# A fourth looked-up tile in the edge-attention pass, and block marks made once per turn

## The reference, cut to what matters

```python
w = softmax(x @ attn_w.T + attn_b);  xp = x + w @ node_anchor
combined = concatenate([x[src], x[dst]], axis=1)
b = softmax(leaky_relu(combined @ edge_w.T + edge_b, 0.01), axis=1)   # (edges, 5)
ep = b @ edge_anchor
agg = zeros_like(xp).at[src].add(ep).at[dst].add(ep)
return xp + 0.5 * agg
```

## Time and profile before

| what | value |
|---|---|
| median of 3 runs | 5374.47 us (5369.51 to 5377.88) |
| profiled execution, its own time | 5368.31 us |
| span of the profiled execution | 5366.5 us |
| busy over the span: PE, POOL, DVE, ACT | 3267.3, 3069.5, 2026.5, 958.0 us |
| mean granted clock of PE over the span | 0.709 |

### The profile page before, as it was taken

One profiled execution on the slowest core, in us unless ns is written; L12 is line 12 of the kernel. 1 busy time (PEld: TensorE's weight loads), 2 busy tenths in 40 slices (PEclk: granted clock), 3 DMA queues, 4 the chain that ended last, 5 costly groups with the idle time before them and its releaser, 6 DMA issues. The chain is left out here.

```text
span 5366.5 us, 69161 instructions
## 1 busy us (share of the span) xinstructions
PE 3267.3 (61%) x19534; PEld 2183.4 (41%) x19535; DVE 2026.5 (38%) x6104; ACT 958.0 (18%) x2127; POOL 3069.5 (57%) x3180
## 2 busy tenths in 40 slices
PE   4357544558997555555554444444479955777777
PEld 2124322234444334334333333333334434666665
DVE  7441101033114322222222222222231157888886
ACT  0010000001003100000000000000010016888885
POOL 5777777730000577777776777777700006777773
PEclk8678767779998655555555555555589966888887
DMA  8521010113224422222222221222232202333322
GB/s 223 144 97 49 24 48 24 48 72 121 96 95 120 115 74 79 80 80 76 80 80 56 52 53 52 52 53 52 51 123 94 96 24 59 68 69 68 67 67 65
DMA packets 370426, 408.73 MB, mean 76 GB/s; under 512 B 89191, under 2 KB 305078, under 8 KB 360374
## 3 DMA queue, kind: packets, MB, share of 16 engines
q1 hardware_dynamic: 268854, 295.73, 17.2%
q0 software_dynamic: 101504, 112.13, 9.7%
HBM read 299.65 MB, written 107.98 MB: 76 GB/s over the span
## 5 line engine op out<-in xcount | busy, mean ns | idle before, releaser
L633 POOL DMA_INDIRECT GS<-xw_table,stage x1664 | 1571.9, 945 | 1182.7 <-issue 1109.9
L1120 PE MATMUL psum<-HA,HT 128*128 128x512 fp8e4 (+1 forms) x5733 | 1211.0, 373 | 458.3 <-DMA HA<-adj 411.6
L1072 PE MATMUL psum<-GS 128*128 128x96 f32 x3328 | 774.1, 409 | 1034.4 <-DMA GS<-xw_table,stage 1014.4
L1072 PEld LDWEIGHTS psum<-GS 128*128 128x128 f32 x3328 | 697.6, 310 | 1110.4 <-issue 1110.4
L633 POOL DMA_INDIRECT HA<-p_table,stage x676 | 652.2, 965 | 750.2 <-ACT stage L916 549.7
L667 POOL DMA_INDIRECT adj<-cell_value,cell_i x832 | 838.5, 1008 | 291.0 <-issue 249.1
L1120 PEld LDWEIGHTS psum<-HA,HT 128*128 128x128 bf16 x5733 | 549.7, 99 | 1093.7 <-issue 456.4
L1577 DVE TENSOR_TENSOR HA<-HA,psum 128x96 f32 x208 | 53.1, 255 | 1357.1 <-PE psum L1072 1357.1
L1563 DVE TENSOR_SCALAR GS<-iota,HT,wt 128x96 f32<-128x96 f32 x1680 | 434.9, 356 | 158.7 <-issue 157.7
L1831 DVE SCALAR_TENSOR_TENSOR GS<-psum,keep,O 128x512 f32<-128x512 f32 (+1 forms) x26 | 18.7, 720 | 1054.3 <-PE psum L1140 737.3
L731 ACT ACTIVATE stage<-cell_i 128x16 int32 (+1 forms) x104 | 22.2, 215 | 1264.9 <-PE psum L1072 1264.9
(11 more groups left out here) (340 smaller groups left out, 3619.0 us busy)
## 6 DMA issues: line engine op xcount, KB each, us to landing
HA<-adj SPq DMA_DIRECT2D x39, 1600.0 KB, 6.5
HA<-adj SPq DMA_DIRECT2D x39, 1536.0 KB, 9.8
HT<-dst_rows SPq DMA_DIRECT2D x212, 256.0 KB
xw_table<-HT SPq DMA_DIRECT2D x100, 512.0 KB, 3.2
adj<-O SPq DMA_DIRECT2D x13, 3136.0 KB, 27.2
GS<-xw_table,stage POOLq DMA_INDIRECT x1664, 2.5
adj<-cell_value,cell_i POOLq DMA_INDIRECT x832
HA<-p_table,stage POOLq DMA_INDIRECT x676
```

The costliest lines, as they stand in the source:

```text
L633: nc.gpsimd.indirect_dma_start(out=to, out_offset=None, in_=table, in_offset=bass.IndirectOffsetOnAxis(ap=idx, axis=0)).then_inc(done, 16)
L1072: last = nc.tensor.matmul(bank[h][:, 0:WINDOW], G3[g][:, j, :], S_pair[h][:, t, :], start=(t == 0), stop=(t == 2 * GT - 1))
L1120: last = nc.tensor.matmul(bank[s][:, 0:w], Hs4[:, b, t, :], adj_tile[s][:, b * GW:b * GW + w], start=(b == 0 and t == 0), stop=(b == SRCS ...
```

## The change

- `LOOKED` goes from 3 to 4: POOL gathers 12 tiles a turn; PE transposes four tiles and looks twelve parts up; ACT copies 512 columns; the fourth look-up fills the second half of bank 6; DVE's two products have 490 columns each and the reduction 980 elements.
- The block marks have two buffers (`hi_l3[0]`, `hi_l3[1]`). `block_columns` makes those of the next turn, at the place where it made those of this turn, and `take_sources` uses their first four tiles. `hi_p` and `source_blocks` are gone.
- In PE's turn the look-ups of groups 1 and 2 stand with `look_up_sources` ahead of the first group of sums, and that of group 3 ahead of the second (before: ahead of the third).
- Some tiles lie elsewhere (`Pp`, `src_rows`, `iota_b`, the second `hi_l3` in GS).

```diff
-LOOKED = 3
+LOOKED = 4
@@ tiles
-        hi_l3 = A[:, 4096:4096 + L16 * 49].rearrange("p (j d) -> p j d", d=49)
+        hi_l3 = [t.rearrange("p (j d) -> p j d", d=49) for t in (A[:, 4096:4096 + L16 * 49], GS[:, 0:L16 * 49])]
-        hi_p = tail[:, 2456:2456 + LOOKED * 49].rearrange("p (j d) -> p j d", d=49)
-        iota_b = tail[:, 2604:2604 + P].bitcast(BF)
+        iota_b = GS[:, 2 * GT * P:2 * GT * P + P].bitcast(BF)
-        looked_p = [bank[7][:, 0:245], bank[7][:, 245:490], bank[6][:, 0:245]]
+        looked_p = [bank[7 - j // 2][:, j % 2 * 245:(j % 2 + 1) * 245] for j in range(LOOKED)]
@@ PE's turn
                     lookup = look_up_logits(it + 1, 1 - u, first + first_blocks(it * 4 + 5, 3))
+                    lookup(1)
+                    look_up_sources(it + 1)
+                    lookup(2)
                     for g in range(4):
-                        if g < 3:
-                            lookup(g + 1)
-                        if g == 0:
-                            look_up_sources(it + 1)
+                        if g == 1:
+                            lookup(3)
                         pe.wait_ge(ready5, it * 4 + g + 1)
@@ DVE
-            def source_blocks(it):
-
-                return V.tensor_tensor(hi_p, iota49.unsqueeze(1).broadcast_to([P, LOOKED, 49]),
-                                       over(src_hi[:, bass.ds(it * L16, LOOKED)], LOOKED, 49), ALU.is_equal)
+            def block_columns(it, u):
+
+                return V.tensor_tensor(hi_l3[u], iota49.unsqueeze(1).broadcast_to([P, L16, 49]),
+                                       over(src_hi[:, bass.ds(it * L16, L16)], L16, 49), ALU.is_equal)
@@ take_sources
-                chosen = hi_p.unsqueeze(2).broadcast_to([P, LOOKED, A5, 49])
-                V.tensor_tensor(products_p[:, 0:2], bank[7][:, 0:490].rearrange("p (j a d) -> p j a d", d=49, a=A5), chosen[:, 0:2], ALU.mult)
-                V.tensor_tensor(products_p[:, 2], bank[6][:, 0:245].rearrange("p (a d) -> p a d", a=A5), chosen[:, 2],
-                                ALU.mult).then_inc(p_taken, 1)
+                chosen = hi_l3[u][:, 0:LOOKED, :].unsqueeze(2).broadcast_to([P, LOOKED, A5, 49])
+                for of, looked in ((slice(0, 2), bank[7]), (slice(2, 4), bank[6])):
+                    last = V.tensor_tensor(products_p[:, of], looked[:, 0:490].rearrange("p (j a d) -> p j a d", d=49, a=A5), chosen[:, of], ALU.mult)
+                last.then_inc(p_taken, 1)
@@ DVE's turn
-                    def block_columns():
+                    def next_block_columns():
 
                         dve.wait_ge(parts5, it + 1)
-                        V.tensor_tensor(hi_l3, iota49.unsqueeze(1).broadcast_to([P, L16, 49]),
-                                        over(src_hi[:, bass.ds(it * L16, L16)], L16, 49), ALU.is_equal)
+                        block_columns(it + 1, 1 - u)
@@ after the soft-max's subtraction
-                    source_blocks(it + 1)
```

More of the change, by code:

```diff
@@ L235, in gnn_stack @@
         products_p = tail[:, 1152:1152 + LOOKED * 245].rearrange("p (j a d) -> p j a d", d=49, a=A5)
-        Pp = tail[:, 1888:1888 + NB * B5 // 2].bitcast(BF)
+        Pp = tail[:, 2132:2132 + NB * B5 // 2].bitcast(BF)
         Pp_part = [Pp[:, t * NB * A5:(t + 1) * NB * A5] for t in range(PARTS)]
-        src_rows = tail[:, 2264:2264 + LOOKED * P // 2].bitcast(BF)
-        hi_p = tail[:, 2456:2456 + LOOKED * 49].rearrange("p (j d) -> p j d", d=49)
-        iota_b = tail[:, 2604:2604 + P].bitcast(BF)
+        src_rows = tail[:, 2508:2508 + LOOKED * P // 2].bitcast(BF)
+        iota_b = GS[:, 2 * GT * P:2 * GT * P + P].bitcast(BF)
         n5 = [T[:, 5300 + i * NB * A5:5300 + (i + 1) * NB * A5].rearrange("p (b a) -> p b a", a=A5) for i in range(3)]
@@ L1703, in rest_attention @@
                         then(V.tensor_scalar(rest_w[:, :], rest_w[:, :], 1.0, None, ALU.subtract))
-                        then(V.tensor_tensor(hi_l3[:, 0:GT, :], iota[:, 0:49].unsqueeze(1).broadcast_to([P, GT, 49]), over(hi4, GT, 49), ALU.is_equal))
+                        then(V.tensor_tensor(hi_l3[0][:, 0:GT, :], iota[:, 0:49].unsqueeze(1).broadcast_to([P, GT, 49]), over(hi4, GT, 49), ALU.is_equal))
                         for j in range(GT):
                             V.tensor_scalar(lo_l3[0][:, j, :], iota[:, 0:P], rest_w[:, j:j + 1], None, ALU.is_equal)
-                            last = V.tensor_tensor(M_l3[:, j, :].rearrange("p (d a) -> p d a", a=A5), over(hi_l3[:, j, :], 49, A5),
+                            last = V.tensor_tensor(M_l3[:, j, :].rearrange("p (d a) -> p d a", a=A5), over(hi_l3[0][:, j, :], 49, A5),
                                                    b5[:, j, :].unsqueeze(1).broadcast_to([P, 49, A5]), ALU.mult)
@@ L2105, in _ @@
             ch(V.tensor_tensor(X3, X3, H3, ALU.add))
-            def source_blocks(it):
-                return V.tensor_tensor(hi_p, iota49.unsqueeze(1).broadcast_to([P, LOOKED, 49]),
-                                       over(src_hi[:, bass.ds(it * L16, LOOKED)], LOOKED, 49), ALU.is_equal)
+            def block_columns(it, u):
+                return V.tensor_tensor(hi_l3[u], iota49.unsqueeze(1).broadcast_to([P, L16, 49]),
+                                       over(src_hi[:, bass.ds(it * L16, L16)], L16, 49), ALU.is_equal)
             def take_sources(it, u):
                 dve.wait_ge(p_looked, it + 1)
-                chosen = hi_p.unsqueeze(2).broadcast_to([P, LOOKED, A5, 49])
-                V.tensor_tensor(products_p[:, 0:2], bank[7][:, 0:490].rearrange("p (j a d) -> p j a d", d=49, a=A5), chosen[:, 0:2], ALU.mult)
-                V.tensor_tensor(products_p[:, 2], bank[6][:, 0:245].rearrange("p (a d) -> p a d", a=A5), chosen[:, 2],
-                                ALU.mult).then_inc(p_taken, 1)
+                chosen = hi_l3[u][:, 0:LOOKED, :].unsqueeze(2).broadcast_to([P, LOOKED, A5, 49])
+                for of, looked in ((slice(0, 2), bank[7]), (slice(2, 4), bank[6])):
+                    last = V.tensor_tensor(products_p[:, of], looked[:, 0:490].rearrange("p (j a d) -> p j a d", d=49, a=A5), chosen[:, of], ALU.mult)
+                last.then_inc(p_taken, 1)
                 dve.wait_ge(p_taken, it + 1)
                 return V.reduce_sum(p_rows[u][:, 0:LOOKED, 0:A5], products_p, AX.X)
-            ch(source_blocks(0))
+            ch(block_columns(0, 0))
             ch(take_sources(0, 0))
@@ L2162, in by_block_and_anchor @@
                         V.tensor_tensor(M_l3[:, at, :].rearrange("p j (d a) -> p j d a", a=A5),
-                                        hi_l3[:, at, :].unsqueeze(3).broadcast_to([P, GT, 49, A5]),
+                                        hi_l3[u][:, at, :].unsqueeze(3).broadcast_to([P, GT, 49, A5]),
                                         b5[:, at, :].unsqueeze(2).broadcast_to([P, GT, 49, A5]), ALU.mult).then_inc(ready5, 1)
@@ L2172, in _ @@
                     dve.wait_ge(logits_done, it + 3)
-                    then(V.scalar_tensor_tensor(z5, z5, 0.01, z5, ALU.mult, ALU.max), block_columns)
+                    then(V.scalar_tensor_tensor(z5, z5, 0.01, z5, ALU.mult, ALU.max), next_block_columns)
                     then(V.reduce_max(m5, z5, AX.X))
                     V.tensor_tensor(z5, z5, over(m5, L16, A5), ALU.subtract).then_inc(soft_in, 1)
-                    source_blocks(it + 1)
                     for g in range(3):
```

## The result

The changed kernel takes 5415.85 us (median of 4 runs, 5415.24 to 5416.54), the kernel before 5375.53 us beside it; the ratio is 1.0073 with a 95% interval of 1.0061 to 1.0084. It is slower by 40.3 us; 5413 us were forecast, 38.5 more than the 5374.47 of the kernel before on record. Its profiled execution has a span of 5414.4 us.

The account below looks back on a forecast made before the run. POOL (16.38 us a turn) and PE (16.32) were both taken as bounds. 50 turns of 0.73 us more, 1.4 and 0.9 make 38.8: 5407.1 us, plus 6.2 from profiled execution to median, 5413; range 5386 to 5424.

Parts of the forecast that it names:

- Two bounds of one length, POOL and PE: Attention pass: POOL's 13 gathers take 16.38 us a turn and PE's serial work 16.32, so both set the pace.
- The gap is PE's own: PE's 3.09 us without matmuls before look-up 1: its sequencer reads block numbers there, rather than waiting for ACT's one-hot rows.
- The size: PE's added work per turn of the attention pass: 0.73 us, paid in full.
- three source look-ups: PE, right behind the gap: three more at 0.202 us each, at a granted clock of 0.50, cost 0.61 us a turn.
- fourth transpose: PE, beside the register loads before look-up 1: may be hidden in part, 0 to 0.18 us a turn, taken as 0.12.
- look-ups moved: PE's look-ups placed earlier among the sums: same 8 matmuls a group, nothing added or taken in PE's order.
- clock on the first sums: PE's first group of sums, mean 2.8 us: a gain from an earlier clock rise was not counted on.
- the rival: PE's clock rises before the first sums, 2.0 us each turn, giving added work back: 5374 to 5380 us, chance 0.09.
- The new wait for the column tile: DVE before writing its columns, until PE's sums by destination free the tile: about 2 us a turn, costing nothing.
- DVE's terms: DVE's two products about 1.17 us and reduction about 1.2; +0.2 us a turn in all, 14.8, hidden.
- What lies outside the 50 turns: First and last turn 0.7 us each, 1.4 together, plus 0.9 for the look-up ahead of the loop.

## Why the prediction was right, and where its sum was not

*Two bounds of one length, POOL and PE.* Shown for POOL: taking 1.65 us of every second turn from PE changes nothing while POOL has 13 gathers, and gives 1.48 us a turn once it has 12. That PE was a bound in the kernel before is read from its trace, in which nothing but its own work and its clock fills a turn. No run took a gather from POOL without giving PE work.

*The gap is PE's own.* Shown by the block numbers: 3.66 us with seven, 2.02 with three, whatever the profile names.

*The size.* 0.73 us a turn was forecast and 0.75 measured. The largest term, the source look-ups, was right. Two others were off, and with the remainder they nearly cancelled out; that the sum agrees to 0.02 us is luck:

| term, us a turn | forecast | measured | from |
|---|---|---|---|
| three source look-ups | +0.61 | +0.62 | 1.80 to 2.42, sources to what follows |
| fourth transpose | +0.12 | about 0 | first transpose to look-up 1: mean 3.65 before, 3.63 after |
| look-ups moved | 0 | about 0 | with four tiles, 17.06 in either order |
| clock on the first sums | 0 | +0.23 | mean 2.89 before, 3.12 after |

The transpose is hidden under the loads, the lower end of its bound. The clock did not give time back, as the rival had it; it took some: every one of the changed kernel's first groups runs 3.0 to 3.2 us, where before they went from 2.0 to 3.3 in a pattern of four turns. The remainder, about -0.1, lies in the later groups: 5.06 us for the three, against 1.78 and 3.40.

The rule of the Trainium skill that was weighed there (TensorE: Matmul & The Clock Gate, Part 1, activity releases the throttle) did not bring the release before the sums in this kernel, whose first sums ran at a granted clock of 0.53 in the turn shown. It came that early in turns of the kernel with fewer loads, where the gap ahead of the work is 1.6 us shorter in every second turn: 0.99 in the first sums shown, 0.85 against 0.80 over the pass. Here it was less idle time ahead, not more work, that came with the higher clock.

*The new wait for the column tile.* There, 1.75 us against "about 2", and without a cost, as forecast: it goes with the old order, and the turn stays 17.06 us. Whether it ends the turn in the kernels with fewer loads was not shown.

*DVE's terms.* 1.27 us for the two products from the first start to the reduction and 1.18 for the reduction, against 1.17 and 1.2.

*What lies outside the 50 turns.* 2.3 us were forecast and about 2.0 measured (39.3 less 37.3).

## What to carry to other kernels

When two engines need the same time for a turn, relieving one of them by giving work to the other loses just that work; look for a gap in the full engine's own timeline before moving anything there. Here it was 3 us of loading and handling block numbers in a row, with four short matmuls ahead to hide under; taking four of seven in every second turn from registers that already held the values, together with the change, made the kernel 0.7% faster than before. And a saving off one bound shows its worth only with the other one lifted: the fewer loads alone measured 0.9999.

## What the runs showed of the hardware

- A block number loaded from SBUF into PE's registers with its register operation and assertion costs PE 0.41 us when no long matmul stands ahead of it ((3.66 - 2.02) / 4). The load instruction took 0.34 us for four numbers, and most of the rest is a register operation (0.15 us) and an assertion for each, one after the other. Behind a group of eight matmuls the four cost nothing (5.06 us for three groups of sums with and without them).
- A shorter gap ahead of PE's work came with nearly twice its length: 0.82 us less gap a turn, and 0.81 us less in the first group of sums, whose granted clock was 0.99 instead of 0.53 in the turns shown.
- On one of the chips the same kernel before took 6515 us instead of 5375. Turns of the pass were some 10 us longer there, with PE, DVE and ACT nearly idle and POOL's gathers going on. The kernels' ratios there ran from 0.999 to 1.027; only that of the kernel before with fewer loads (0.999) agreed with its ratio elsewhere (0.9999).
